# Feed-forward of a decoder layer: both first-layer weights of a 64-unit chunk side by side in one stationary tile

## The reference

```python
logits = xf @ gate_w.T
probs = softmax(logits); topk_p, topk_i = top_k(probs, 2)
h1 = einsum('nc,eic->eni', xf, w1); h2 = einsum('nc,eic->eni', xf, w2)   # 8 experts of 352 units
y  = einsum('enc,ne->nc', einsum('eni,eci->enc', silu(h1) * h2, w3), comb)
sh = silu(xf @ sw1.T) * (xf @ sw2.T) @ sw3.T                              # shared expert, 704 units
x  = x + y + sh
```

## Time and profile before

| | |
|---|---|
| timed runs (3) | 1194.95, 1196.88, 1198.07 us; median 1196.88 |
| profiled execution, its own time | 1200.02 us |
| its span | 1198.3 us |
| TensorE busy | 978.5 us (82% of the span) |
| VectorE, ScalarE, GpSimd busy | 834.3, 646.0, 271.8 us |
| mean granted TensorE clock | 0.967 |

### The profile page before, as it was taken

How to read it: one execution, slowest core, us unless ns; L and a number is a source line. 1 busy time by engine, 2 the same in 40 slices (tenths; PEclk the granted TensorE clock), 3 DMA queues, 4 the chain that set the end, 5 groups by cost and what they waited for, 6 DMA issues and landing times. The chain is left out here.

```text
span 1198.3 us, 21781 instructions
## 1 busy us (share of the span) xinstructions
PE 978.5 (82%) x8049; PEld 667.7 (56%) x8049; DVE 834.3 (70%) x1398; ACT 646.0 (54%) x1040; POOL 271.8 (23%) x265
## 2 busy tenths in 40 slices
PE   4988987999877677767777767675889899999996
PEld 3744835888654444444444444444667666556665
DVE  6858656899888999999999999997634321111225
ACT  3453362455677888888888888885133012121220
POOL 1135054566407700000000000002524500000032
PEclk9999999999987999999999999998979899999998
DMA  8400002110000100000000000000040792221134
GB/s 315 167 1 1 1 1 105 55 36 19 8 1 1 46 1 1 0 0 0 0 0 0 0 0 0 0 0 1 24 157 2 292 404 89 83 102 62 62 93 145
DMA packets 24858, 68.19 MB, mean 57 GB/s; under 512 B 2722, under 2 KB 6818, under 8 KB 23778
## 3 DMA queue, kind: packets, MB, share of 16 engines
q1 hardware_dynamic: 20114, 52.48, 11.7%
q0 software_dynamic: 4400, 14.42, 3.7%
q10 hardware_dynamic: 288, 0.52, 0.2%
HBM read 49.07 MB, written 18.35 MB: 56 GB/s over the span
## 5 line engine op out<-in xcount | busy, mean ns | idle before, releaser
L1317 ACT ACTIVATE cs_p_int<-cs_s_b,cs_bias,cs_step_now 128x1024 int16<-128x1024 f32 x128 | 154.0, 1203 | 63.8 <-DVE cs_bias L1352 63.8
L1345 DVE TENSOR_REDUCE cs_top<-cs_s_b 128x1 f32<-128x512 f32 x256 | 164.7, 685 | 12.3 <-PE cs_s_b L1374 3.4
L1374 PE MATMUL cs_s_b<-k_parts,q_int 96*128 96x512 bf16 x256 | 80.0, 395 | 110.5 <-ACT cs_p_int L1317 110.4
L1382 PE MATMUL cs_tp<-ident,cs_p_int 128*128 128x128 f16 x2048 | 159.4, 222 | 2.9 <-ACT cs_pT L1323 1.1
L1333 DVE TENSOR_REDUCE cs_top<-cs_s_a 128x1 f32<-128x1024 f32 x128 | 155.5, 1215 | 4.3 <-PE cs_s_a L1374 4.3
L1317 ACT ACTIVATE cs_p_int<-cs_s_a,cs_bias,cs_step_now 128x1024 int16<-128x1024 f32 x128 | 152.8, 1194 | 0.0
L1382 PEld LDWEIGHTS cs_tp<-ident,cs_p_int 128*128 128x128 f16 x2048 | 121.6, 98 | 48.5 <-issue 44.7
L2198 PE MATMUL ff_h<-ff_experts,ff_zgT 128*128 x368 | 112.9, 460 | 0.9 <-ACT ff_zgT L1837 0.9
L1480 POOL TENSOR_TENSOR co_o<-co_o,v_step 128x512 f32<-128x512 f32 x8 | 10.6, 1330 | 414.3 <-DVE co_o L1502 414.3
L1374 PE MATMUL cs_s_a<-k_parts,q_int 96*128 96x512 bf16 x256 | 80.3, 396 | 22.7 <-ACT cs_p_int L1317 17.9
L1360 DVE COPY cs_pT<-cs_tp 128x1024 int16<-128x1024 int16 x128 | 87.1, 680 | 3.3 <-PE cs_tp L1382 3.1
(11 more groups left out here) (287 smaller groups left out, 2120.7 us busy)
## 6 DMA issues: line engine op xcount, KB each, us to landing
ff_experts<-in_experts_dram SPq DMA_DIRECT2D x8, 2176.0 KB, 14.1
slots<-sa_zero SPq DMA_DIRECT2D x1, 5888.0 KB, 24.9
ff_zg<-slots POOLq DMA_DIRECT2D x23, 256.0 KB, 2.9
run_y<-ff_yv SPq DMA_DIRECT2D x23, 256.0 KB, 2.0
ff_raw<-in_weights_dram SPq DMA_DIRECT2D x6, 768.0 KB, 5.2
ck_raw<-in_ctxT_dram SPq DMA_DIRECT2D x8, 512.0 KB, 3.2
stage<-in_cwkv_dram SPq DMA_DIRECT2D x2, 1024.0 KB, 5.1
out_dram<-x_res SPq DMA_DIRECT2D x8, 256.0 KB, 2.0
```

What stands on the lines that cost most here:

```text
L1317: nc.scalar.activation(p_int[:, u, half * HALF:(half + 1) * HALF], s[:, :], ACT.Exp, bias=bias[:, u:u + 1], scale=step_now[:, h:h + 1], ac ...
L1345: nc.vector.tensor_reduce(top[:, u, 1 + c:2 + c], s_b[:, c * 512:(c + 1) * 512], AX_X, ALU.max).then_inc(max_ok, 1)
L1374: ins = nc.tensor.matmul(s[:, c * 512:(c + 1) * 512], q_int[0:3 * D, t, h, :], k_parts[0:3 * D, h, keys:keys + 512], start=True, stop=True)
L1382: ins = nc.tensor.transpose(tp[:, k, :], p_int[:, u, key:key + P].bitcast(F16), ident16[:, :])
```

## The change

The sixth chunk (c = 5) is no longer filled up in the first layer. Its 64 columns of `sw1` and its 64 of `sw2` stand side by side in one 128-column stationary tile, so 12 matmuls in place of 24 for each half of the tokens give `h1` on partitions 0 to 63 and `h2` on partitions 64 to 127 of one bank. Silu reads the lower half, VectorE multiplies it by the upper half; the wait for `h2_ok` is gone for this chunk. All element-wise work of the chunk covers 64 partitions, the split of its first-layer weights half the columns, and the second layer contracts over 64 rows. The loads are as large as before (the place of `sw2` is zero).

```diff
+TAIL = SHARED_W - (SHARED - 1) * P
+assert 2 * TAIL == P
...
+        def rows_of(c):
+            return P if c < SHARED - 1 else TAIL
+
+        def up_parts(c):
+            return 2 if c < SHARED - 1 else 1
...
-                nc.scalar.copy(up_hi(c).rearrange("p a k n -> p (a k n)"), raw(c)[:, 0:2 * C]).then_inc(uhi_ok, 1)
+                width = up_parts(c) * C
+                nc.scalar.copy(up_hi(c).rearrange("p a k n -> p (a k n)")[:, 0:width], raw(c)[:, 0:width]).then_inc(uhi_ok, 1)
...
-                    nc.scalar.activation(act_s(c)[:, b, :], h1[b][:, :], ACT.Silu).then_inc(s_ok, 1)
+                    rows = slice(0, rows_of(c))
+                    nc.scalar.activation(act_s(c)[rows, b, :], h1[b][rows, :], ACT.Silu).then_inc(s_ok, 1)
...
+                rows = rows_of(c)
+                gates = h2[b][:, :] if rows == P else h1[b][rows:2 * rows, :]
                 v_.wait_ge(s_ok, n + 1)
-                v_.wait_ge(h2_ok, n + 1)
+                if rows == P:
+                    v_.wait_ge(h2_ok, n + 1)
...
-                nc.vector.tensor_tensor(g(c)[:, b, :], act_s(c)[:, b, :], h2[b][:, :], ALU.mult).then_inc(g_ok, 1)
+                nc.vector.tensor_tensor(g(c)[0:rows, b, :], act_s(c)[0:rows, b, :], gates, ALU.mult).then_inc(g_ok, 1)
...
-                for m, (out, made) in enumerate(((h1, h1_ok), (h2, h2_ok))):
+                for m, (out, made) in enumerate(((h1, h1_ok), (h2, h2_ok))[0:up_parts(c)]):
...
+                        rows = slice(0, rows_of(c))
                         for i, (hh, w) in enumerate(((h_hi, dn_hi), (h_lo, dn_hi), (h_hi, dn_lo))):
-                            ins = nc.tensor.matmul(py[t % 2][:, :], hh(c)[:, tile], w(c),
+                            ins = nc.tensor.matmul(py[t % 2][:, :], hh(c)[rows, tile], w(c)[rows, :],
                                                    start=(q == 0 and i == 0), stop=(q == GROUP - 1 and i == 2))
...
+    last = [u[SHARED - 1].reshape(P, CK, P) for u in up]
+    both = np.concatenate([w[:, :, 0:TAIL] for w in last], axis=2).reshape(P, C)
+    up = [np.concatenate([u[0:SHARED - 1], w[None]]) for u, w in zip(up, (both, np.zeros_like(both)))]
```

More of the change, by code:

```diff
@@ L1819, in split_up @@
                     act.wait_ge(h2_ok, 2 * c - 2)
-                nc.scalar.copy(up_hi(c).rearrange("p a k n -> p (a k n)"), raw(c)[:, 0:2 * C]).then_inc(uhi_ok, 1)
+                width = up_parts(c) * C
+                nc.scalar.copy(up_hi(c).rearrange("p a k n -> p (a k n)")[:, 0:width], raw(c)[:, 0:width]).then_inc(uhi_ok, 1)
             def split_down(c):
-                nc.scalar.copy(dn_hi(c), raw(c)[:, 2 * C:3 * C]).then_inc(dhi_ok, 1)
+                nc.scalar.copy(dn_hi(c)[0:rows_of(c), :], raw(c)[0:rows_of(c), 2 * C:3 * C]).then_inc(dhi_ok, 1)
             def hidden(c):
@@ L1828, in hidden @@
                     act.wait_ge(h1_ok, n + 1)
-                    nc.scalar.activation(act_s(c)[:, b, :], h1[b][:, :], ACT.Silu).then_inc(s_ok, 1)
+                    rows = slice(0, rows_of(c))
+                    nc.scalar.activation(act_s(c)[rows, b, :], h1[b][rows, :], ACT.Silu).then_inc(s_ok, 1)
                     act.wait_ge(g_ok, n + 1)
-                    nc.scalar.copy(h_hi(c)[:, b * HALF_T:(b + 1) * HALF_T], g(c)[:, b, :]).then_inc(hhi_ok, 1)
+                    nc.scalar.copy(h_hi(c)[rows, b * HALF_T:(b + 1) * HALF_T], g(c)[rows, b, :]).then_inc(hhi_ok, 1)
             def turned(u):
@@ L2016, in low_hidden @@
                 cols = slice(b * HALF_T, (b + 1) * HALF_T)
-                nc.vector.tensor_tensor(h_lo(c)[:, cols], g(c)[:, b, :], h_hi(c)[:, cols].bitcast(F32),
+                rows = slice(0, rows_of(c))
+                nc.vector.tensor_tensor(h_lo(c)[rows, cols], g(c)[rows, b, :], h_hi(c)[rows, cols].bitcast(F32),
                                         ALU.subtract).then_inc(late_hlo_ok, 1)
@@ L2021, in low_down @@
                 v_.wait_ge(dhi_ok, c + 1)
-                nc.vector.tensor_tensor(dn_lo(c), raw(c)[:, 2 * C:3 * C], dn_hi(c).bitcast(F32),
+                rows = slice(0, rows_of(c))
+                nc.vector.tensor_tensor(dn_lo(c)[rows, :], raw(c)[rows, 2 * C:3 * C], dn_hi(c)[rows, :].bitcast(F32),
                                         ALU.subtract).then_inc(late_dlo_ok, 1)
@@ L2026, in low_up @@
                 v_.wait_ge(uhi_ok, c + 1)
-                nc.vector.tensor_tensor(up_lo(c).rearrange("p a k n -> p (a k n)"), raw(c)[:, 0:2 * C],
-                                        up_hi(c).rearrange("p a k n -> p (a k n)").bitcast(F32),
+                width = up_parts(c) * C
+                nc.vector.tensor_tensor(up_lo(c).rearrange("p a k n -> p (a k n)")[:, 0:width], raw(c)[:, 0:width],
+                                        up_hi(c).rearrange("p a k n -> p (a k n)")[:, 0:width].bitcast(F32),
                                         ALU.subtract).then_inc(late_ulo_ok, 1)
```

## The result

The changed kernel took 1207.88 us (median of four runs, 1207.33 to 1209.91) against 1196.13 for the kernel before (four runs, 1194.95 to 1198.07): a ratio of 1.0098, interval [1.0081, 1.0115], so 9.7 to 13.8 us **slower**. The forecast was 1193.8 with a range up to 1199.5. The profiled execution, one of the four, took 1209.91 us; its mean granted clock is 0.955 where it was 0.967.

What follows compares the result with a forecast made beforehand. The end was taken as bound by when `down(2)` may start and how long its 48 matmuls take; -4.8 (first layer) + 1.2 (64 rows) + 0.5 (clock) = -3.1 us, median 1196.88 to 1193.8, own range 1192 to 1196, all cases 1191.3 to 1199.5.

Steps and rivals of the forecast that it cites:

- the clock's: TensorE's clock falls in the wait before `down(2)` and returns after it: +0.5 us, ends 0 and +1.1.
- The rows' price: In `down(2)`, changes between 128 and 64 rows cost +0.09 going in, +0.11 coming out: 1.5 us at that end.
- the stall: In `down(2)` TensorE waits for VectorE; this takes up 0.27 us of the cost of changing rows.
- Rival 2: In `down(2)`, 64 rows cost nothing, as 96: -4.3 us, 1192.6; chance 0.2.
- the sum's +1.2: The term for the second layer's 64 rows in `down(2)`, +1.2 us in the sum.
- the eight-row group: Matmuls of eight rows whose spacing (0.32 us going in, 0.34 on return, against 0.227) priced the 64 rows.
- The first layer: 24 matmuls fewer in chunk 5; VectorE's queue then sets the start of `down(2)`, 1176.86 for 1181.65: -4.8 us.
- the late completion: First-layer results of chunk 5 seen 2.2 to 3.9 us after TensorE's records end; seen once more near 950 us.
- rival 1: The late completion is absent from timed runs: start only -0.9, slow side +2.4 to +3.5 us; chance 0.32, half slow.
- the late spots: End of first layer and near 950 us: with clock losses 12.6 us together, held against rival 1.

Runs made afterwards that it cites:

- after: The changed kernel itself, as profiled after the change, against the kernel before; 1207.88 us, ratio 1.0098.
- before_down64: The kernel before with only the second layer of chunk 5 on 64 rows, first layer not merged; 1206.55 us, ratio 1.0072.
- pad_tiny64: merge_pad128 with one small matmul of 64 rows and 32 columns ahead of each group of three in `down(2)`; 1217.36 us in one execution.
- early_rows64: early_pad128 with chunk 5's second layer on 64 rows, its first 18 matmuls behind the wait all of 64 rows; 1200.81 us in one execution.
- all64: The changed kernel with every matmul of `down(2)` on 64 rows, leaving out chunk 4's upper 64 units; 1203.95 us in one execution.
- after_warm: The changed kernel with 24 matmuls of 128 rows into an unread bank before `down(2)`; seven executions, 1194.29 to 1208.50 us.
- after_again: The changed kernel run again without an edit, in the fourth set; 1208.67 us, ratio 1.0118 to the kernel before.
- merge_pad128: The changed kernel with chunk 5's second layer on 128 rows, padded with zero weights; 1195.75 us, ratio 0.9997 to the kernel before.
- after_warm_again: after_warm repeated without an edit in another set; 1196.99 us, ratio 1.0011 to the kernel before, ten executions between 1194.28 and 1199.76.
- merge_rows96: The changed kernel with 96 rows in chunk 5's second layer, rows 64 to 95 of the weights zero; 1199.34 us in one execution.
- before_again: The kernel before, unchanged, run for a second profile of its end; 1193.89 us.
- before_third: The kernel before, unchanged, run and profiled once more in the fourth set; 1195.58 us.
- pad_warm: merge_pad128 with 24 matmuls of 128 rows into an unread bank behind the first layer; 1194.67 us, ratio 0.9947 to the kernel before.
- pad_tiny128: merge_pad128 with one small 128-row, 32-column matmul ahead of each group of three in `down(2)`; 1201.36 us in one execution.
- early_pad128: merge_pad128 with chunk 4's second-layer matmuls for six tiles done while VectorE still works on chunk 5; 1191.93 us, ratio 0.9977 to the kernel before.
- pad_warm_again: pad_warm repeated without an edit in another set; 1193.60 us, ratio 0.9983 to the kernel before.
- early_again: early_pad128 repeated without an edit in the fourth set; 1190.48 us, ratio 0.9968 to the kernel before.
- pad_late_mix: merge_pad128 with mixes 3 and 4 moved behind the last remainder and mixes 5 to 7 behind additions; 1195.12 us, ratio 0.9985 to the kernel before.

## Why the prediction was wrong

**The step that failed: the clock's.** The prediction put "+0.5, with 0 and +1.1 as ends". It took for granted that the clock returns after 4 to 6 us, since both rows it had the earlier trace rows show that; in both TensorE was at matmuls of 128 rows, a condition that it did not ask about. With 64 rows among them it returned in none of the seven profiles that had lost it (after, before_down64, pad_tiny64, early_rows64, all64, after_warm, after_again). At 0.427 a matmul, 48 cost 20.5 us in place of 10.9: **+9.6**, and the changes cost more at the lower level too. No rival had a clock that stays down, so the range could not hold the result. In all64 TensorE worked on 64 rows for 20.83 us without a break and the granted clock read 0.50 to the end; in merge_pad128, after a wait as long as the changed kernel's, 3.1 us on 128 rows were enough.

**The rows' price, half the size.** The prediction read +0.09 going in and +0.11 coming out and counted each once, 1.5 us in all. The after's rows show that every change, of either direction, stretches two intervals, the one before it and the one behind it: 0.10 each at full clock (before_down64, after_warm_again), 15 x 0.20 = 3.0, less the 0.27 of the stall, against 2.75 measured in after_warm_again. At the lower level it is 0.29 a change, 4.4 us. Rival 2, that 64 rows cost nothing, holds for 96 rows only (spacing 0.43 us at 0.50 and 0.23 at full clock, changes included, in merge_rows96). No run shows the sum's +1.2 for the 64 rows: it carried the spacing of the eight-row group over to them, which was the author's estimate. In its place the runs showed 2.75 us for the 15 changes at full clock, and 4.4 less the 0.3 of the stall at 0.50.

**The first layer.** 24 matmuls fewer, g(5,0) behind mix 2, g(5,1) behind mix 4, `down(2)` 2.3 us behind it, 4.8 sooner than in the profiled execution: each of these steps came out. What was wrong is what they were held against. The profiled execution of the kernel before had the late completion; two others did not (before_again, before_third), and its timed median of 1196.13 is that of the sets without it. There the start is only 0.96 sooner. The prediction had this as rival 1 at 0.32, and weighed against it that the late spots would cost 12.6 us together while the runs lie only 2 to 5 us lower. That argument failed twice. In the sets without late results the kernel before still varies from 1192.5 to 1201.2 us, too much to rule it out by totals. And the 6.6 us near 950 must not be added: without the late result TensorE stands a little later anyway, for the tokens that the routed experts gather. Chain of waits of before_again:

```profile
952.39 8.85 DMA ff_zg<-slots
...
961.29 1.04 PE ff_pc L2186 x4
```

Its clock falls after that wait (4.33 us) and is back at 968.2; in the profiled execution of the kernel before, the late result comes in its place. The first layer of chunk 4 then starts at 1153.64 there and at 1153.24 in before_again, 0.4 apart. What the late results cost is what they cost at the end, (28.01 - 24.13) + (13.43 - 11.57) = 5.7 us, and the two executions differ by 1200.02 - 1193.89 = 6.1.

**The sum, corrected**, for a chip without late results: start -0.96, `down(2)` 25.28 - 11.57 = +13.7, together +12.7 us. Measured are 9.7 to 13.8. By parts: the clock +9.6, the changes +4.4, the stall they cover -0.3, the start -1.0.

**Where late results occur** the merge should be worth its 4.8 us: the late waits of all64 delay `down(2)` by only 0.3 us (it starts 23.45 behind the first layer, 23.17 elsewhere), since mixes 3 and 4 lie over them, and pad_warm gained 6.6 there, the clock's part included. This is argued, not shown: merge_pad128 and the changed kernel themselves were not run in that set. Nearest to it is pad_tiny128, the merge with 16 small matmuls: its `down(2)` took 16.1 us in place of 13.0, so without them its 1201.36 would be about 1198.3, some 3 below the kernel before, an estimate from one execution. The cause of the late results is not known. That it goes with the chip is only what five sets suggest, and the profiled execution of the kernel before had them while its timed ones, by their times, did not.

## What to carry to other kernels

A matmul over 64 rows was not a cheap matmul over 128 here: both start every 0.427 us at a clock of 0.50 (all64, merge_pad128), each change cost 0.2 us at full clock and 0.29 at 0.50, and once the clock had fallen it stayed at 0.50 for the rest of a `down(2)` with such matmuls (25.28 us in the changed kernel, 20.83 in all64). Padding chunk 5 with zeros to 128 rows took the whole loss away (merge_pad128, 1195.75 us against 1195.81); 96 rows, in one execution, let the clock return too, after 3.8 us. When an edit shortens one engine's work but another sets the restart, the wait only grows (2.37 us in before_again, 6.82 in merge_pad128): fill it with work that is due anyway (early_pad128, ratios 0.9977 and 0.9968, a gain of 0.2 to 0.3%), and before trusting a stall that the profile ascribes to nothing, look for it in a second execution.

## What the runs showed that was not expected

- 64-row matmuls of 512 columns, packed at 0.427 us, leave the granted clock at 0.50 for 20.83 us (all64); matmuls of 128 or 96 rows bring it back 3.0 to 6.2 us after the restart of `down(2)`. One 64-row matmul of 32 columns among four is enough to keep it down (pad_tiny64 1217.36, against pad_tiny128 1201.36).
- From full clock it fell within some 2 us of the restart under 64-row matmuls (before_down64 after a wait of 2.37 us, after_warm after 1.37), where the same waits ahead of 128 rows left it up (before_again, before_third, pad_warm, pad_warm_again). But after_warm fell by its times in two of seven executions and then in none of ten, so a share of chance in these pairs is not ruled out.
- Few rows are not harmful as such: between 160 and 182 us the kernel before runs 32-row matmuls for 8.5 us, several at once (eight of 512 columns within 1.1 us), between others of 128 rows, and the clock stays at 1.00.
- In `down(2)` waits of 2.4 us ahead of 128-row matmuls left the clock at 1.00 (before_again, before_third), waits of 2.6, 3.9 and 6.8 did not (early_pad128 and early_again, pad_late_mix, merge_pad128).
